# Router scores with tokens on partitions instead of experts: eight short matmuls a chunk for two long ones, without the transposes

## What is computed

```python
def _L1_ffn_ref(x, A, B, Wr):
    K, TOPK, RANK = (64, 16, 16)
    xf = x.reshape(-1, x.shape[-1])
    scores = xf @ Wr.T                                   # 2048 x 64
    top_vals, top_idx = jax.lax.top_k(scores, TOPK)
    gates = jax.nn.softmax(top_vals, axis=-1)
    G = jnp.zeros((N, K), xf.dtype).at[jnp.arange(N)[:, None], top_idx].set(gates)
    h = jnp.einsum('nd,krd->nkr', xf, A)
    out = jnp.einsum('nkr,kdr->nd', h * G[:, :, None], B)
    return (out * SCALING).reshape(*prefix, -1)
```

## Time and profile before

| | |
|---|---|
| three executions, median | 661.34 us (660.93 to 661.41) |
| the profiled execution, its own time | 659.91 us |
| its span, first to last instruction | 658.1 us |
| PE busy | 649.5 us, 99% of the span |
| weight loads (PEld) busy | 537.6 us, 82% |
| DVE / ACT / POOL busy | 451.2 / 213.5 / 72.9 us |
| granted TensorE clock | 1.0 throughout: the level of 2.4 GHz |
| HBM | 240 GB/s over the span |

### The profile page before, as it was taken

How to read it: one execution, slowest core, us unless ns; L and a number is a source line. 1 busy time by engine, 2 the same in 40 slices (tenths; PEclk the granted TensorE clock), 3 DMA queues, 4 the chain that set the end, 5 groups by cost and what they waited for, 6 DMA issues and landing times.

```text
span 658.1 us, 8354 instructions
## 1 busy us (share of the span) xinstructions
PE 649.5 (99%) x3197; PEld 537.6 (82%) x3197; DVE 451.2 (69%) x690; ACT 213.5 (32%) x275; POOL 72.9 (11%) x91
## 2 busy tenths in 40 slices
PE   9999999999999999999999999999999999999997
PEld 8878888888897788888789788888879888888875
DVE  2859469549378888558779648636867856665775
ACT  2714235315134024335124312334423421433420
POOL 1499300000000160000000042000000000000000
PEclk9999999999999999999999999999999999999999
DMA  8587714984988836776985682274987665037685
GB/s 314 196 292 279 296 49 135 356 247 167 392 280 346 336 149 255 272 225 251 366 296 186 266 319 96 101 225 161 366 323 268 259 252 190 0 116 206 223 333 215
DMA packets 51450, 157.98 MB, mean 240 GB/s; under 512 B 5472, under 2 KB 6368, under 8 KB 51424
## 3 DMA queue, kind: packets, MB, share of 16 engines
q1 hardware_dynamic: 46096, 148.05, 62.0%
q10 hardware_dynamic: 5328, 9.61, 4.8%
HBM read 131.94 MB, written 25.71 MB: 240 GB/s over the span
## 4 chain that ended last, share of the span: by engine, by line
PE 74%; DMA 12%; DVE 7%; issue 2%; ACT 2%; SPq 1%; ACTq 0%; DVEq 0%
PE bank L1367 19%; PE bank L1369 19%; PE bank L1368 19%; PE bank L1381 7%; DMA gate_x<-gates 5%; DMA piece_lo<-kept 4%; PE bank L1401 3%; DMA raw<-pieces 2%; PE bank L1388 2%; PE bank L1393 1%; PE bank L1407 1%; PE bank L1395 1%; DMA toep<-taps 1%; PE bank L1408 1%; DVE x L918 1%
## 5 line engine op out<-in xcount | busy, mean ns | idle before, releaser
L886 DVE TENSOR_TENSOR piece_lo<-raw,piece_hi 128x1024 fp32r<-128x1024 f32 x60 | 74.2, 1240 | 90.1 <-ACT piece_hi L639 89.8
L639 ACT ACTIVATE piece_hi<-raw 128x1024 fp32r<-128x1024 f32 x60 | 63.3, 1057 | 143.9 <-PE bank L1369 100.5
L1367 PE MATMUL bank<-piece_hi,u_hi 128*128 128x512 f32 x272 | 107.9, 397 | 0.1
L1369 PE MATMUL bank<-piece_hi,u_lo 128*128 128x512 f32 x272 | 107.3, 394 | 0.0
L1368 PE MATMUL bank<-piece_lo,u_hi 128*128 128x512 f32 x272 | 107.3, 394 | 0.0
L1367 PE MATMUL bank<-v_hi,piece_hi 128*128 128x512 f32 x256 | 101.8, 398 | 0.0
L1369 PE MATMUL bank<-v_hi,piece_lo 128*128 128x512 f32 x256 | 101.1, 395 | 0.0
L1368 PE MATMUL bank<-v_lo,piece_hi 128*128 128x512 f32 x256 | 101.0, 394 | 0.0
L1367 PE MATMUL bank<-piece_hi,v_hi 128*128 128x512 f32 x192 | 76.2, 397 | 1.1 <-DMA piece_lo<-kept 1.0
L1369 PE MATMUL bank<-piece_hi,v_lo 128*128 128x512 f32 x192 | 75.8, 395 | 0.0
L1368 PE MATMUL bank<-piece_lo,v_hi 128*128 128x512 f32 x192 | 75.8, 395 | 0.0
(11 more groups left out here) (143 smaller groups left out, 799.2 us busy)
## 6 DMA issues: line engine op xcount, KB each, us to landing
raw<-pieces SPq DMA_DIRECT2D x76, 512.0 KB, 5.3
piece_hi<-kept SPq DMA_DIRECT2D x48, 512.0 KB, 4.7
piece_lo<-kept SPq DMA_DIRECT2D x48, 512.0 KB, 6.1
conv_in<-conv_x SPq DMA_DIRECT2D x16, 516.0 KB, 6.8
x<-x SPq DMA_DIRECT2D x16, 512.0 KB, 5.4
gate_x<-gates ACTq DMA_DIRECT2D x32, 256.0 KB
out<-x SPq DMA_DIRECT2D x32, 256.0 KB, 4.4
conv_in<-pieces SPq DMA_DIRECT2D x12, 512.0 KB, 8.6
```

The lines of the kernel that those rows point to most:

```text
L639: act.activation(piece_hi[:, n % SLOTS, :], raw[:, r % RAWS, :], ACT.Copy).then_inc(s_piece_hi, 1)
L886: dve.tensor_tensor(piece_lo[:, n % SLOTS, :], raw[:, r % RAWS, :], piece_hi[:, n % SLOTS, :].bitcast(F32), ALU.subtract).then_inc(s_piece ...
L1367: pe.matmul(to, left_hi, right_hi, start=first, stop=False)
L1369: return pe.matmul(to, left_lo, right_hi, start=False, stop=last)
```

## The change

In `score` the roles are exchanged: the activations are the weights (four blocks of 128 tokens), and wr_r, 128 columns, is the moving side. A chunk now takes eight matmuls of 128 moving columns instead of two of 512. The result arrives with tokens on partitions, in the layout that the transposes made. So `score_out` on ACT, `score_transposed` on PE and the semaphores `s_score` and `s_score_t` go; the last score matmul raises `s_score_n`, on which DVE's `choose` waits, and `choose` reads bank 4 (first group) or 5 (others) instead of 5 or 1. `start` is set once in a bank, at the first block of the first chunk.

```diff
-        lora_h, score_t, gate_t = small, small, small[0:KR_E, :]
+        lora_h, gate_t = small, small[0:KR_E, :]
...
-            def score_out(g, bank):
-                act.wait_ge(s_score, g + 1)
-                act.activation(score_t[:, :], banks[bank][:, :], ACT.Copy).then_inc(s_score_t, 1)
...
                 split_first(11)
-                score_out(0, 4)
                 gates_exp(0)
...
-                score_out(g, 5)
                 next_split(16)
                 gates_exp(g)
...
-                choose(0, 5)
+                choose(0, 4)
...
-                choose(g, 1)
+                choose(g, 5)
...
             def score(g, i, c, bank):
                 split_done(g, MIX0 + i)
-                pe.matmul(banks[bank][:, :], wr_r[:, c, :], v_hi[:, c, :], start=(i == 0), stop=False)
-                mm = pe.matmul(banks[bank][:, :], wr_r[:, c, :], v_lo[:, c, :], start=False, stop=(i == NCH - 1))
+                for t in range(NT):
+                    cols = slice(t * P, (t + 1) * P)
+                    pe.matmul(banks[bank][:, cols], v_hi[:, c, cols], wr_r[:, c, :], start=(i == 0 and t == 0),
+                              stop=False, skip_group_check=True)
+                    mm = pe.matmul(banks[bank][:, cols], v_lo[:, c, cols], wr_r[:, c, :], start=False,
+                                   stop=(i == NCH - 1), skip_group_check=True)
                 if i == NCH - 1:
-                    mm.then_inc(s_score, 1)
+                    mm.then_inc(s_score_n, 1)
...
-            def score_transposed(g, bank):
-                pe.wait_ge(s_score_t, g + 1)
-                for t in range(NT):
-                    mm = pe.transpose(banks[bank][:, t * P:(t + 1) * P], score_t[:, t * P:(t + 1) * P], ident)
-                mm.then_inc(s_score_n, 1)
...
-                h_of(1, (0,))
-                score_transposed(0, 5)
-                h_of(1, order[1:])
+                h_of(1, order)
...
-                h_of(1, (0,))
-                score_transposed(g, 1)
-                h_of(1, range(1, NCH))
+                h_of(1, range(NCH))
```

More of the change, by code:

```diff
@@ L214, in adaln_ffn_kernel @@
         s_lo = sem("s_lo")
-        s_score = sem("s_score")
-        s_score_t = sem("s_score_t")
         s_score_n = sem("s_score_n")
```

## The result

Over five runs of each, the changed kernel takes 675.42 us median (675.15 to 676.13), the kernel before 660.93 (659.44 to 661.41). The ratio is 1.0228, with a 95% interval of 1.0211 to 1.0245: 2.3% slower, 14 to 16 us. The forecast was +10.3 us. The sign and the main term held, and the size was short by 4 to 6 us. The range given, 668 to 675.5 us, ends 14.2 us above the 661.3 that it was reckoned from; the change cost 14.5 us by the medians and 15.1 by the ratio, just past that end.

What follows compares the result with a forecast made beforehand. PE was taken as the bound. Scores +13.8, transposes -1.8, absorbed waits -0.7 and -1.0 sum to +10.3 us, on the 661.3 us median giving 671.6 us, 1.6% slower; range 668 to 675.5 us.

Steps and rivals of the forecast that it cites:

- the main term: Scores in the mixing stages: +0.432 us a chunk, 32 times, +13.8 us.
- What bounds the kernel: PE, busy throughout the mixing stages of groups 2, 3 and 0; more PE work there moves the end later.
- The price of a score matmul: Each 128-column score matmul taken at 0.112 us, the pace of weight loads; eight replace two of 0.232.
- A: Rival in the score runs: columns pace, loads hide, only the transposes' gain is left, 659.5 us; chance 0.05.
- B: Rival in the score runs: load and matmul don't overlap, 0.170 us each, 686.5 us; chance 0.06.
- C: Rival in the score runs: fp32r matmuls have a floor near 0.232 us, about 702 us; chance 0.07.
- Step 2: Four PE transposes a group go, 0.45 us a group: -1.8 us.
- Step 3: ACT's score copy, 0.60 us a group, lay beside PE work; removing it gains nothing.
- Step 4: Start of DVE's choice: the 2.75 us (group 2) or 1.88 us (group 0) delay goes, worth nothing by itself.
- Step 5: Group 1's PE waits for DVE absorbed by a later PE: -0.7 us before scores, -1.0 in the convolution.
- All other stretches unchanged: Expected sign: outside the stretches the prediction named, the profile stays as before.

Runs made afterwards that it cites:

- lo_half: Changed kernel with the v_lo score matmuls taking only the router's high part, 64 moving columns: 676.72 us against 659.66 for the kernel before, ratio 1.0268.
- interleaved: Changed kernel with each chunk's score matmuls spread in pairs between the long h matmuls: 675.69 us, ratio 1.0231 to the kernel before.
- first_new: Kernel before with the new scores in group 0 alone, groups 1 to 3 old: 665.73 us against 659.66, ratio 1.0089.
- shifted: Changed kernel with idle waits in group 0 making its program 195 instructions longer there, so the loop's code starts further on: 673.37 us, ratio 1.0207 to the kernel before.
- fetch_first: Changed kernel with the two last weight pieces issued ahead of group 1's four loads of next weights: 673.80 us against 659.54 for the kernel before, ratio 1.0206.
- hi_only: Changed kernel without the scores' v_lo matmuls, four a chunk instead of eight: 660.75 us against 659.54 for the kernel before, ratio 1.0022.
- pad88: Kernel before with 92 more instructions, idle waits, in the PE's loop body: 660.97 us against 659.66, ratio 1.0019.
- loop_new: Kernel before with the new scores in the loop alone (groups 1 to 3), group 0 old: 668.94 us against 659.66, ratio 1.0141.
- pad_both: Kernel before with 92 idle waits in group 0 and 92 in the loop body: 664.55 us against 659.90, ratio 1.0062.
- pad_first: Kernel before with 92 idle waits in group 0's PE code only: 662.04 us against 659.90, ratio 1.0029.
- the two remedies together: Changed kernel with both the 195 instructions of waits in group 0 and the earlier weight-piece fetches: 672.04 us against 660.15 for the kernel before, ratio 1.0177.

## Where the prediction was right, and the step that failed

- **What bounds the kernel: right.** What the PE is given more of in the mixing stages, the end gets later by; the stage of group 2 is 3.03 us longer.
- **The price of a score matmul: right.** 0.112 us assumed, 0.109 to 0.114 measured, +0.43 a chunk 32 times. The witness was the load that followed another by 0.12 in the earlier trace rows. lo_half shows that columns don't pace, since 64 fewer change nothing; interleaved, with 0.06 between two short matmuls while the loads keep 0.11, speaks for the load and against a fixed cost.
- **Rivals A, B, C: all fell** by the same rows. A needs under 0.065 us a matmul, B 0.170, C 0.232. By the Trainium skill, page "TensorE: Matmul & The Clock Gate", section "Back-to-back issue gap", the pairs would come 81 ns apart; this trace has 112. The rule of the same page, section "The mechanism", that loads overlap only where the row group differs, would have given B: the loads here, all 128 rows each, start while the matmul ahead of them runs (88.34 inside the matmul of 88.29), so this trace disagrees.
- **Step 2, transposes: mis-sized a little.** -0.45 a group assumed, -0.39 measured, +0.25 us in all.
- **Step 3, ACT's copy at nothing: nothing speaks against it.** No wait of PE for ACT came or went.
- **Step 4, the shorter chain at nothing: right as to the PE.** DVE starts 2.8 us sooner behind the last score and nothing on the PE gains from it.
- **Step 5, absorbed waits: half right.** The -0.7 at the scores of group 1 came as forecast. The -1.0 in group 1's convolution did not: the stalls there grew by 0.5. The step took DVE's chain to be late by its own 1.5 us against the PE's 3.0. In the trace the choice of group 0 is late by 2.1 (98.75 for 96.67, 0.4 of it from the start), but the chain is 3.5 us late by 150 us and 4.1 by 190: between, it takes buffers that the PE gives back and waits for transfers, which would hand the PE's delay on to it; that is argued, not tested. The stalls vary from profile to profile (0.23 us in first_new, none in shifted, 0.6 idle in fetch_first, 1.2 idle in hi_only where the PE isn't later at all). They are missing even in the profiles of pad88 and loop_new, which have the old code up to that point; pad88, timeline of PE, the whole convolution in one run:

```profile
179.98 14.45 PE L1392 MATMUL bank<-toep,conv_in 128*128 128x128 f32 x128
```

  So the code up to there doesn't fix the two stalls of the earlier trace rows, and one profile of them was no ground for a term of -1.0. What sets them stays open.
- **"All other stretches unchanged": wrong, and the step that failed.** Of the 5.8 us between +10.3 and the profiled +16.1, 3.4 to 3.5 stand here and 1.5 in step 5. The prediction counted every instruction that the change adds as work for the engine and none as code. 88 instructions more in group 0 and 88 in the loop's body made the PE fetch its loop again in each pass (two stalls, 2 us in sum) and put one packet of code into a full stretch of the DMA queue, where a weight piece came late (1.45 us). That the code does this is shown by pad_both, which has the matmuls of before and both kinds of stall; by shifted, in which the edge stalls are gone; and for the late weight piece by pad_first. How much of the 1.45 us is code is less sure, since 0.84 and 0.43 us of stall remain in shifted. Taking both stalls out of the changed kernel gives back 14.5 - 11.9 = 2.6 us by the medians, 3.4 by the ratios.

The balance of medians: 11.9 us for the new scores (10.3 forecast; 0.25 of the difference from the transposes and up to 1 from stalls that didn't close), and 2.6 to 3.4 us for the edge stalls and the late piece. Only the two remedies together are clear of the noise; each alone is worth about 1.4 us by the ratios, with overlapping intervals. Runs of one kernel scatter by about 1 us either way, so nothing finer can be read.

## What to carry to other kernels

Where a matmul's moving side gets as narrow as its weights (128 columns here), count weight loads, not columns: putting the narrow operand on the moving side only pays if the loads have a longer matmul each to hide behind. Instructions that a change adds are also code: compare the packets of the instruction queue and where they fall, and when a gap opens at a loop's edge, test it with waits that have long passed, in the old kernel, before believing the releaser that the profile names. A stall that looks like slack to be absorbed may hang on the engine that you are delaying, or may be there in one execution and not in the next: read it in a second profile before it becomes a term of a sum.
